# A state-space scan between two feed-forward layers: rings of three units of decays and five of states, and sums and gates one unit earlier

## The reference

```python
x_ssm, z = jnp.split(h @ Win, 2, axis=-1)          # 512 inner channels each
x_ssm = silu(depthwise_conv4(x_ssm) + conv_b)
dt = softplus(x_ssm @ dt_w + dt_b)
Bt, Ct = x_ssm @ Bp, x_ssm @ Cp                    # 64 states
state = state * exp(dt_t * A) + (dt_t * x_t) * B_t # for every token, channel and state
y_t = sum over states of state * C_t
y = (y + x_ssm * D) * silu(z)
out = x + y @ Wout
```

## Time and profile before

| | |
|---|---|
| median of 3 runs | 5407.56 us (5406.04 to 5408.29) |
| the profiled execution | 5437.24 us |
| its span, first to last instruction | 5435.4 us |
| busy: PE matmul / weight load / DVE / ACT / POOL | 4912.3 / 2809.6 / 4876.0 / 3903.0 / 5021.1 us |
| scans (DVE) | 4096, 4633.2 us |
| products with C (POOL) | 2048, 4785.3 us |
| first scan | 171.3 us after the span's start |
| granted TensorE clock, mean | 0.987 |

### The profile page before, as it was taken

The page is one execution under the profiler, slowest core; times in us unless marked ns, Lnnn a source line. Parts: engine busy times, 40 slices in busy tenths (PEclk is TensorE's granted clock), DMA queues, the critical chain, the costliest instruction groups (busy, mean ns, idle before and its releaser), DMA issues.

```text
span 5435.4 us, 189342 instructions
## 1 busy us (share of the span) xinstructions
PE 4912.3 (90%) x85070; PEld 2809.6 (52%) x85070; DVE 4876.0 (90%) x4595; ACT 3903.0 (72%) x6659; POOL 5021.1 (92%) x2310
## 2 busy tenths in 40 slices
PE   4798999999999999999999999998999999999887
PEld 2455555555555555555555555555555555555554
DVE  1699899999999989999899999989999999998996
ACT  4777777767778777787777778677777777766564
POOL 0699899999999999999999999999999999999997
PEclk8899999999999999999999999999999999999998
DMA  6475665756557565665656556575565756656553
GB/s 174 161 178 188 169 191 179 174 196 173 196 174 186 184 166 197 172 190 184 170 193 171 198 176 184 185 168 197 173 185 186 174 194 168 191 178 164 197 182 119
DMA packets 578860, 976.04 MB, mean 180 GB/s; under 512 B 294881, under 2 KB 328450, under 8 KB 510466
## 3 DMA queue, kind: packets, MB, share of 16 engines
q1 hardware_dynamic: 313858, 961.82, 56.2%
q10 hardware_dynamic: 264192, 2.11, 3.2%
HBM read 875.74 MB, written 88.08 MB: 177 GB/s over the span
## 4 chain that ended last, share of the span: by engine, by line
PE 35%; DVE 26%; POOL 24%; issue 9%; DMA 3%; ACT 2%; SPq 0%; ACTq 0%; DVEq 0%; another core or an unknown queue 0%; POOLq 0%
DVE H L528 24%; POOL H L618 22%; PE pUB L685 12%; PE Y L709 10%; PE pP L643 4%; PE pP L649 4%; PE pA L740 2%; DMA Bd<-scratch_diag 2%; PE pA L734 2%; DVE cv L479 2%; ACT dA L362 1%; POOL duo L605 1%; POOL dto L599 1%; DMA Cb<-scratch_c 1%; POOL lnv L594 1%
## 5 line engine op out<-in xcount | busy, mean ns | idle before, releaser
L618 POOL TENSOR_TENSOR H<-H,Cb 128x1024 f32<-128x1024 f32 x2048 | 4785.3, 2391 | 233.4 <-DVE H L528 221.3
L528 DVE TENSOR_TENSOR_SCAN H<-dA,pUB 128x512 f32<-128x512 f32 x4096 | 4633.2, 1198 | 373.7 <-PE pUB L685 325.7
L362 ACT ACTIVATE dA<-DT,w_negA 128x512 f32<-128x512 f32 x4096 | 2619.0, 710 | 1310.0 <-DVE H L528 1300.7
L685 PEld LDWEIGHTS pUB<-Bd,UT 64*64 64x64 f32 x65536 | 1875.6, 133 | 1909.9 <-DVE H L528 1065.0
L685 PE MATMUL pUB<-Bd,UT 64*64 64x128 f32 x65536 | 2243.2, 274 | 413.1 <-DVE H L528 326.1
L709 PE MATMUL Y<-H,w_ident 64*64 64x512 f32 x16384 | 2176.5, 600 | 5.0 <-POOL H L618 3.3
L709 PEld LDWEIGHTS Y<-H,w_ident 64*64 64x64 f32 x16384 | 519.4, 133 | 298.5 <-issue 246.2
L643 PE MATMUL pP<-hT,w_Win 128*128 128x512 f32 x512 | 263.4, 638 | 16.1 <-DVE cv L479 11.7
L649 PE MATMUL pP<-U,w_dt_w 128*128 128x512 f32 x512 | 263.9, 641 | 6.6 <-DVE absv L542 4.8
L362 ACT ACT_TABLE_LOAD x178 | 228.4, 1283 | 3.2
L479 DVE SCALAR_TENSOR_TENSOR cv<-pP,w_conv_w,cv 128x511 f32<-128x511 f32 (+2 forms) x192 | 139.2, 725 | 31.8 <-ACT cv L300 31.6
(11 more groups left out here) (80 smaller groups left out, 1619.7 us busy)
## 6 DMA issues: line engine op xcount, KB each, us to landing
Cb<-scratch_c SPq DMA_DIRECT2D x512, 1024.0 KB, 5.3
Bd<-scratch_diag SPq DMA_DIRECT2D x512, 512.0 KB, 5.9
scratch_diag<-H SPq DMA_DIRECT2D x16, 1024.0 KB, 15.2
scratch_z<-zo SPq DMA_DIRECT2D x64, 256.0 KB, 5.9
scratch_dt<-dto SPq DMA_DIRECT2D x64, 256.0 KB, 8.3
scratch_ut<-uto SPq DMA_DIRECT2D x64, 256.0 KB, 7.4
DT<-scratch_dt SPq DMA_DIRECT2D x64, 256.0 KB, 5.4
UT<-scratch_ut SPq DMA_DIRECT2D x64, 256.0 KB, 6.0
```

The source lines that it names most:

```text
L362: last = nc.scalar.activation(dA[:, n % DAR, j, :], DT[:, k, :], ACT.Exp, scale=c["negA"][:, k, GS * blk + j:GS * blk + j + 1])
L528: last = nc.vector.tensor_tensor_scan(H[:, u % HR, 2 * i + j, :], dA[:, n % DAR, 2 * i + j, :], pUB[:, i, :].rearrange("p (t s) -> p s t", ...
L618: nc.gpsimd.tensor_tensor(h[:, j:j + 2, :], h[:, j:j + 2, :], Cb[:, blk % 2, j:j + 2, :], ALU.mult).then_inc(times_c, 1)
L685: last = nc.tensor.matmul(out, UT[rows, k, j * P + h * HP:j * P + h * HP + HP], Bd[rows, blk % 2, i, j * P:(j + 1) * P].rearrange("p (t s) ...
```

## The change

- The ring of decays has three units, the ring of states five. The slot of a decay is now counted over all units and not within the sequence (64 is no multiple of three). The two rings take eight units of 8 KB a partition together, as before.
- A pair's sum has two blocks of two rows of states: the first half in unit p + 2, the second in p + 3, each behind the second force of its unit. Before it had four single rows in units p + 3 and p + 4.
- On PE `other` stands between the two forces in every unit.
- The gates go from units 3 and 35 to units 2 and 34.
- The tables of the timetable have new numbers. The order of the pieces of one kind is kept; they are spread over more of the step. Long pieces on PE (four or eight matmuls of 512 or 256 columns) stood at units 0, 3 to 12, 15, 18, 19, 24, 25, 30, 31, 36, 37, 42, 43 (y at 5, 6, 9, 10) and stand now at 0, 3, 5, 7, 8, 10, 12, 13, 15, 17 to 20, 22, 26, 28, 32, 34, 40, 42, 48, 50 (y at 7, 12, 17, 19). Convolutions on DVE were at units 2, 6, 10, 14 and are at 2, 7, 12, 17. POOL's dt work began at 29, 35, 41, 47 and begins at 32, 38, 46, 54.

```diff
-DAR, HR = 2, 6
+DAR, HR = 3, 5
...
-PES = {"xs": (0, 4, 8, 12), "z": (3, 7, 11, 15), "BC": ((18, 19),), "turn b": (22,), "dt": ((24, 25), (30, 31), (36, 37), (42, 43)),
+PES = {"xs": (0, 5, 10, 15), "z": (3, 8, 13, 18), "BC": ((20, 22),), "turn b": (24,), "dt": ((26, 28), (32, 34), (40, 42), (48, 50)),
...
-                            last = nc.scalar.activation(dA[:, n % DAR, j, :], DT[:, k, :], ACT.Exp,
+                            last = nc.scalar.activation(dA[:, (GN * b + n) % DAR, j, :], DT[:, k, :], ACT.Exp,
...
-                if close and n == 3 and i == 1:
+                if close and n == 2 and i == 1:
                     gate(c_, 2)
                     gate(c_, 3)
-                if scan and n == HALF + 3 and i == 1:
+                if scan and n == HALF + 2 and i == 1:
...
-                                last = nc.vector.tensor_tensor_scan(H[:, u % HR, 2 * i + j, :], dA[:, n % DAR, 2 * i + j, :],
+                                last = nc.vector.tensor_tensor_scan(H[:, u % HR, 2 * i + j, :], dA[:, u % DAR, 2 * i + j, :],
...
+            def add_states(b, n, half):
+
+                pe.wait_ge(times_c, at(2 * (GN * b + n + 1) + half + 1))
+                for j in (2 * half, 2 * half + 1):
+                    for r in range(2):
+                        rows = slice(r * HP, r * HP + HP)
+                        for i in range(2):
+                            last = nc.tensor.matmul(Y[r][i * HP:i * HP + HP, :], c["ident"][rows, rows], H[rows, (GN * b + n + i) % HR, j, :],
+                                                    start=False, stop=(n % HALF == HALF - 2 and j == GS - 1))
+                if half:
                     last.then_inc(summed, 2)
...
+            def sum_states(b, n, scan, close):
+
+                p, half = (n - 2, 0) if n % 2 == 0 else (n - 3, 1)
...
                     if proj and n + 1 == GN:
                         force(b + 1, 0, 0)
-                    if n % 2:
-                        other(b, n, close, proj, ffn)
-                    sum_states(b, n, 0, scan, close)
+                    other(b, n, close, proj, ffn)
                     if scan and n + 1 < GN:
                         force(b, n + 1, 1)
                     if proj and n + 1 == GN:
                         force(b + 1, 0, 1)
-                    if n % 2 == 0:
-                        other(b, n, close, proj, ffn)
-                    sum_states(b, n, 1, scan, close)
+                    sum_states(b, n, scan, close)
```

More of the change, by code:

```diff
@@ L27 @@
 AX = mybir.AxisListType
-SPS = {"load x": (0,), "load 2": (10, 14), "load 0": (50, 54), "load r": (2,), "store z": (6, 10, 14, 18), "store C": (22,), "store dt": (31, 37, 43, 49),
-       "store u": (37, 43, 49, 56), "load z": (28, 29, 36, 37), "store out": (48,), "store r": (42,)}
-ACTS = {"tap": (2, 6, 10, 14), "u": (5, 9, 13, 17), "z": (5, 9, 13, 17), "BC": (21,), "B": (24,),
[3 rows of a table removed]
-DVES = {"norm 1": (4,), "norm c": (19,), "norm 2": (35,), "norm 3": (47,), "soft": (28, 34, 40, 46),
-        "conv": (2, 6, 10, 14), "x2": (8, 12), "x1": (23, 29), "out": (41, 47)}
-POOLS = {"dt": (29, 35, 41, 47), "du": (30, 36, 42, 48)}
-PES = {"xs": (0, 4, 8, 12), "z": (3, 7, 11, 15), "BC": ((18, 19),), "turn b": (22,), "dt": ((24, 25), (30, 31), (36, 37), (42, 43)),
-       "turn u": (34, 40, 46, 52), "turn 1": (13, 16), "turn c": (32, 35), "turn 3": (51, 54)}
-LATER = {"y": ((5, 6), (9, 10)), "ffn 1": ((20, 21), (26, 27)), "ffn c": ((38, 39), (44, 45))}
+SPS = {"load x": (0,), "load 2": (10, 14), "load 0": (46, 54), "load r": (2,), "store z": (6, 12, 16, 22), "store C": (26,),
+       "store dt": (34, 40, 48, 56), "store u": (42, 50, 58, 62), "load z": (28, 29, 36, 37), "store out": (48,), "store r": (52,)}
+ACTS = {"tap": (2, 7, 12, 17), "u": (5, 10, 15, 20), "z": (5, 10, 15, 20), "BC": (24,), "B": (26,),
[3 rows of a table added]
+DVES = {"norm 1": (6,), "norm c": (26,), "norm 2": (43,), "norm 3": (51,), "soft": (31, 37, 45, 53),
+        "conv": (2, 7, 12, 17), "x2": (13, 20), "x1": (30, 34), "out": (44, 46)}
+POOLS = {"dt": (32, 38, 46, 54), "du": (33, 39, 47, 55)}
+PES = {"xs": (0, 5, 10, 15), "z": (3, 8, 13, 18), "BC": ((20, 22),), "turn b": (24,), "dt": ((26, 28), (32, 34), (40, 42), (48, 50)),
+       "turn u": (38, 46, 54, 59), "turn 1": (23, 25), "turn c": (36, 39), "turn 3": (56, 60)}
+LATER = {"y": ((7, 12), (17, 19)), "ffn 1": ((27, 29), (31, 33)), "ffn c": ((41, 43), (44, 45))}
 EL = P * T
@@ L700, in skip_over @@
                 last.then_inc(skip, 1)
[L702 to L711, removed]
-                    last.then_inc(summed, 2)
[L714 to L723, removed]
+            def add_states(b, n, half):
[7 more added lines that the diff above has]
+                if half:
+                    last.then_inc(summed, 2)
             def transpose(i, done):
@@ L813, in other @@
                         transpose(i, t2)
+            def sum_states(b, n, scan, close):
+                p, half = (n - 2, 0) if n % 2 == 0 else (n - 3, 1)
+                if scan and p >= 0:
+                    if p % HALF == 0 and half == 0:
+                        skip_over(b, p)
+                        skip_over(b, p + 1)
+                    add_states(b, p, half)
+                if close and p < 0:
+                    add_states(b - 1, GN + p, half)
             def step(b, scan, close, proj, ffn):
```

## The result

The changed kernel takes 5371.4 us (5357.0 to 5372.3), the kernel before 5406.0 on the same chip (5395.9 to 5408.3): a ratio of **0.9932** (95% interval 0.9919 to 0.9945), 0.7% faster, 35 us. The forecast was 84 us less, 5323. The direction was right and the time lies in the range, but the gain is less than half of what was forecast.

What follows compares the result with a forecast made beforehand. A step was taken as POOL's work plus idle time, 327.2 = 312.9 + 14.3 us. Idle falling to 8.7 saves 5.6 a step, 84 us over fifteen steps; 5407.6 - 84 gives 5323, range 5245 to 5395.

Steps and rivals of the forecast that it cites:

- What bounds the kernel: Whole step: 327.2 us is POOL's work 312.9 plus idle 14.3; the change pays only what it takes from idle.
- PE's order: Units 8 to 31: a long piece costs DVE 0.65 us instead of 0.78, so the stretch takes 120.6, against 125.3.
- Units 0 to 7: Start of the step: 43.3 us against 43.7, including a new 0.7 us wait of the moved gates for the sum.
- POOL's stock: Lag of POOL at the step's end limited to 8.2 us, not 10.1; stock 5.7, not 7.6, costing 1.9 a step.
- Units 32 to 63: Second half of the step: POOL needs 165 us, DVE 153; POOL sets the pace and is never idle.
- ACT: Units 42 to 53: crowded, 59 us of work against POOL's 59.7; fits with the longer lead as cover, counted as nothing.
- The queues: SP's list: same transfers, each store still a unit or more behind the work it stores; nothing added.
- From the trace to the median: Whole run: the 84 us saving counted from the 5437.2 us profiled execution was subtracted from the unprofiled median, 5407.6.
- Order gives nothing: Rival for units 8 to 31: PE's pieces cost what they did, 125.3 us, 14 us saved in all, 5394; chance 0.10.
- The slower rival: Units 8 to 31: the block of two sums holds the next force, 1.2 us a piece, 5447; chance 0.12.

Runs made afterwards that it cites:

- e2: The changed kernel with the old timetable, keeping new rings, sum blocks, gates and place of the pieces: 5414.4 us, ratio 1.0021.
- e3: The kernel before with the new timetable alone: 5378.4 us, ratio 0.9953.
- e6: The changed kernel with eight products nothing reads added on PE in unit 2 of steps 1 to 14: 5338.6 us, ratio 0.9884.
- e7: The changed kernel with the first feed-forward's second half at units 30 and 31, its addition at 32 instead of 34: 5351.6 us, ratio 0.9902.
- e4: The changed kernel with rings of two units of decays and six of states: 5356.3 us, ratio 0.9918.
- e1: The kernel before, unchanged, run again for a second trace: median 5403.6 us, profiled execution 5407.3 us.
- e8: The changed kernel with the gates one unit later, at 3 and 35: 5390.7 us, ratio 0.9980.
- e5: The changed kernel with the first convolution in unit 3 instead of 2 and first z projection in 4 instead of 3: 5347.9 us, ratio 0.9897.

## Why the prediction was right or wrong, point by point

- *What bounds the kernel: a step is POOL's work and POOL's idle time.* Right. POOL's work was 312.9 us in the step counted, and its mean over steps 1 to 14 lies between 313.4 and 314.4 in every trace; all gains and losses above are its idle time.
- *PE's order.* Right in kind. The count gave 0.5 us for a piece, which I raised to 0.65 by the ratio found before. That step was wrong on the safe side: units 8 to 31 take 118.9 us, which is 112.8 and 0.5 for each of twelve pieces. e2 and e3 show what I had not separated: half of the 6.8 us comes from the order, half from the spread. The 1.7 us that this term was too dear hid the error of the next one: units 0 to 31 were forecast at 163.9 us and took 163.8, by luck.
- *Units 0 to 7: 43.3 us.* **Wrong, and the first step that failed: a mechanism that had no term.** They took 44.9. It priced the gates' move by one wait of 0.7 us on DVE. That wait is there (0.32 in unit 2, 1.41 in unit 34 of the step shown). What it left out is what the crowded unit of DVE does to PE: 4.06 us without work, then 4.5 us of products at 1.2 GHz, a stall of 2.59 us for DVE, and it did not count the skip product behind the force either. The trace of before has the clock at 1.00 in all four stretches, and I read that as a property of the kernel when it was one of its order. e6 prices it at 33 us: 2.6 us of POOL's idle time in each of 14 steps. The Trainium skill (TensorE: Matmul & The Clock Gate, Part 1) says that the throttled clock is the default and that activity releases it; the trace agrees (0.54 behind the wait, 1.00 there once e6 fills it).
- *POOL's stock: a lag of 8.2 us in place of 10.1.* Right in what the lag becomes: its mean at the end of a step is 8.3 us, with PE waiting for POOL at the sum (64.4 us in all, 3.3 before). The 10.1 was one step's; the mean before is 9.1, so the limit moved by 0.8 us and not by the 1.9 that I counted: again an error on the safe side. In single units the price is higher: behind a wait of 2.30 us at the sum in unit 57 the clock fell too (0.67 in the 3.58 us from 2412.92). Such falls in units 57 to 60 are not new: six steps of the first trace before have one, seven of the changed kernel.
- *Units 32 to 63.* **The second step that failed: a wait put at nothing.** In units 48 to 63 POOL is never idle, as predicted, but in 32 to 47 it is idle 1.7 us on the average (1.0 in the step shown) where nothing was forecast; the second trace before has 0.4 there. The wait of the gates at unit 34 was put at no cost. Unit 34 lasts 8.3 us and empties POOL's stock; e7 prices it at 20 us.
- *ACT.* Right that nothing comes of the crowd. The reason was wrong: the longer lead was not needed as a cover for units 42 to 53, as e3 and e4 show with a lead of one.
- *The queues.* ACT's copy of the turned product in unit 61 waits 132.8 us in all, in 16 steps, for the store of the one before, which stands in SP's queue behind the wait for POOL. I had said that each store stands behind its work and not asked who waits for the store. It costs nothing (e4, with one unit of lead, shows no loss).
- *From the trace to the median.* **The third step that failed, and the largest share of the miss.** I took the 30 us between the profiled execution and the median for a constant. They were 2 us of POOL's idle time in each step: 14.3 were counted, 12.3 are there in e1. More than a third of the 5.6 us a step that the change was to take away was not there in the other executions.

The missing 49 us, counted in POOL's idle time of a step: 2.0 us lie in the base (14.3 counted, 12.3 in e1), 1.3 in the changed step (8.7 forecast, 10.0 measured); 3.3 x 15 = 50 us. So the base is three fifths of the miss. The clock's loss alone, 2.6 us a step, is twice what the changed step missed, and unit 34 comes on top; the two terms that were too dear, a piece and POOL's limit, made up for the rest. The forecast of the changed step was nearer than its mechanism deserved.

The same by lengths: a step of before is 325.8 us (e1), the changed one was forecast at 321.6 (320.9 in e6, without the clock's loss): 4.2 x 15 = 63 us. Measured it is 323.7: 2.1 x 15 = 32 us; between the two spans (5405.4 and 5370.4) lie 35.0, so 3.5 come from the rest of the program, which I had at nothing. Between the medians: 35.

Of the rivals none came. "Order gives nothing" falls: the order is worth 3.2 to 3.6 us in units 8 to 31, though 2.0 us of that are lost again in units 0 to 7 (44.9 against e3's 42.9). The Trainium skill's rule (Perfetto Trace Analysis, Identifying the Most-Contended Engine), which judges TensorE's headroom by weight loads and MFU and by which PE had slack at weight loads of 52% (54% now), gave that rival's time, and the runs speak against it here. The slower rival named a neighbouring mechanism (a block that holds the next force) in the wrong stretch; in units 8 to 31 it does not happen. Its 44.9 for units 0 to 7 is what was measured, but it came from pieces at 1.2 us, not from the clock.

## What to carry to other kernels

When work of two kinds is moved into one slot of an engine, ask which other engine has nothing to do in that slot, and how it comes back: a PE that waited 2.6 to 4.1 us at one place ran what followed at half clock in many steps or in all, and the work right behind the wait is the most urgent. Where PE waits anyway, filler products can be cheaper than the wait. A saving that is taken from idle time has to be checked against a second execution of the kernel before, since idle time is what differs between executions.

## What the runs showed of the hardware that was not expected

- PE's granted clock fell to 1.2 GHz behind the wait of unit 2 (4.06 us in the step shown) in all fifteen steps, though PE worked before and after it. In e8 two waits, of 2.43 and 2.2 to 3.0 us, stand in units 2 and 3, and it fell in every step; behind one of 2.6 to 2.8 us (e5) it fell in nine of fourteen. In unit 57, waits of 2.30 and 2.42 us for POOL were followed by it and one of 2.41 was not.
- The same program's ACT waited 46.6 us for no visible cause at one kind of instruction in one execution and 12.6 in another, enough to move a step by 2 us.
- With 52 us of filler products PE was busy 16 us longer in all (4859.6 and 4843.9), and the kernel took 0.6% less time.
